# A layer of gated linear attention and a four-layer FFN: the order of TensorE's work at the end of a half, and how sums of squares are formed

## The reference, cut to what matters

```python
xn = _layernorm(x)                                   # x: 16 x 512 x 256
x = x + attn(xn) + ffn(xn)

# attn (Di = 512, K = 64)
u = xn @ up_w.T ; final_gate = xn @ gate_w.T
shift = silu(causal_conv4(u) + conv_b)
q, k = shift @ q_w.T, shift @ k_w.T
o = gla_chunk_scan(q * SCALE, kn, v, rt_log)         # gated linear attention
o = o + shift * residual_weight
xg = o * silu(final_gate)
rms = rsqrt(mean(xg * xg, axis=-1) + 1e-5)
attn = (xg * rms * norm_weight) @ down_w.T           # 512 -> 256

# ffn (ternary weights, 256 -> 1024 -> 1024 -> 1024 -> 256)
h = silu(xn @ w1.T * s1) * (xn @ w2.T * s2)
h = gelu(h @ h1.T * sh1)
h = gelu(h @ h2.T * sh2)
ffn = h @ w3.T * s3
```

## Time and profile before

| | us |
|---|---|
| median of 3 runs | 1945.26 (1943.17 to 1946.41) |
| the profiled execution | 1944.75 |
| its span on the core | 1943.0 |
| TensorE busy | 1926.5 (99%) |
| VectorE busy | 1586.9 (82%) |
| ScalarE busy | 1296.4 (67%) |
| GpSimd busy | 81.2 (4%) |
| one half in the loop | about 58.9 |

### The profile page before, as it was taken

The page is one execution under the profiler, slowest core; times in us unless marked ns, Lnnn a source line. Parts: engine busy times, 40 slices in busy tenths (PEclk is TensorE's granted clock), DMA queues, the critical chain, the costliest instruction groups (busy, mean ns, idle before and its releaser), DMA issues.

```text
span 1943.0 us, 46120 instructions
## 1 busy us (share of the span) xinstructions
PE 1926.5 (99%) x16804; PEld 1907.6 (98%) x16804; DVE 1586.9 (82%) x4304; ACT 1296.4 (67%) x2687; POOL 81.2 (4%) x136
## 2 busy tenths in 40 slices
PE   8999999999999999999999999999999999999998
PEld 7999999999999999999999999999999999999998
DVE  7788888888788887888888788787888878878887
ACT  5676667766676766666766677675667666667565
POOL 0000000000000000000000000000000000000000
PEclk9999999999999999999999999999999999999999
DMA  8000000000000000000000000000000000000000
GB/s 308 7 12 12 12 2 12 12 12 12 12 1 12 12 12 12 11 2 12 12 12 12 7 7 12 12 12 12 1 12 12 12 12 12 1 12 12 13 7 8
DMA packets 23538, 34.19 MB, mean 18 GB/s; under 512 B 3170, under 2 KB 19810, under 8 KB 23364
## 3 DMA queue, kind: packets, MB, share of 16 engines
q1 hardware_dynamic: 23364, 31.43, 4.8%
HBM read 23.04 MB, written 8.39 MB: 16 GB/s over the span
## 4 chain that ended last, share of the span: by engine, by line
PE 95%; issue 2%; ACT 1%; DVE 1%; SPq 1%; DMA 0%; POOLq 0%; POOL 0%; DVEq 0%; ACTq 0%
PE fb L383 65%; PE ab L383 21%; PE ab L593 2%; PE ab L628 1%; PE ab L529 1%; PE ab L518 1%; PE ab L453 1%; PE ab L583 1%; PE fb L679 1%; SPq L289 0%; PE ab L590 0%; PE ab L469 0%; ACT wwhole L727 0%; PE ab L606 0%; DMA shift<-stage_w 0%
## 5 line engine op out<-in xcount | busy, mean ns | idle before, releaser
L383 PE MATMUL fb<-hid1h,wwhole 128*128 128x256 f32 x2048 | 474.7, 279 | 0.0
L383 PE MATMUL fb<-hid1l,wwhole 128*128 128x256 f32 x2048 | 468.5, 276 | 0.0
L383 PE MATMUL fb<-hid0l,wwhole 128*128 128x256 f32 x2048 | 465.9, 276 | 0.0
L383 PE MATMUL fb<-hid0h,wwhole 128*128 128x256 f32 x2048 | 465.8, 276 | 0.0
L383 PEld LDWEIGHTS fb<-hid1h,wwhole 128*128 128x128 f32 x2048 | 384.6, 188 | 3.9 <-ACT raw L839 0.2
L383 PEld LDWEIGHTS fb<-hid1l,wwhole 128*128 128x128 f32 x2048 | 384.7, 188 | 0.0
L383 PEld LDWEIGHTS fb<-hid0h,wwhole 128*128 128x128 f32 x2048 | 384.4, 188 | 0.0
L383 PEld LDWEIGHTS fb<-hid0l,wwhole 128*128 128x128 f32 x2048 | 384.4, 188 | 0.0
L839 ACT ACTIVATE raw<-fb,sh_s 128x256 f32<-128x256 f32 x512 | 212.9, 466 | 143.2 <-PE fb L383 135.1
L383 PE MATMUL fb<-xntl,wwhole 128*128 128x256 f32 x1024 | 237.5, 276 | 0.0
L383 PE MATMUL fb<-xnth,wwhole 128*128 128x256 f32 x1024 | 237.5, 276 | 0.0
(11 more groups left out here) (234 smaller groups left out, 4527.3 us busy)
## 6 DMA issues: line engine op xcount, KB each, us to landing
xin<-x SPq DMA_DIRECT2D x32, 256.0 KB, 2.6
out<-xin SPq DMA_DIRECT2D x32, 256.0 KB, 2.2
stage_more<-stage_w SPq DMA_DIRECT2D x6, 512.0 KB, 7.3
sgate<-stage_w SPq DMA_DIRECT2D x4, 512.0 KB, 4.7
shift<-stage_w SPq DMA_DIRECT2D x4, 512.0 KB, 5.4
v<-stage_w SPq DMA_DIRECT2D x4, 512.0 KB, 5.6
raw<-stage_w SPq DMA_DIRECT2D x3, 512.0 KB, 6.1
mixed<-stage_w SPq DMA_DIRECT2D x3, 512.0 KB, 8.4
```

The lines of the kernel that those rows point to most:

```text
L383: mm = pe.matmul(o, a, b, start=start and i == 0, stop=stop and i == len(pairs) - 1)
```

## The change

On TensorE w3 goes directly behind h2. The four transposes of the next input follow it, and behind them, in the same group, two new transposes that bring `sqsum` (128 features by 128 tokens, twice) to 128 tokens by 128 features in `fb[1]`. The two matmuls with ones behind the down projection are gone. VectorE sums what the two transposes leave over the free dimension (`total`), and forms `msq` from that.

On ScalarE the squares are formed in two pieces of 128x512, ahead of `ln_high`. On VectorE three additions take the place of the reduction over the four squares, and they stand ahead of `ln_low`; `total` and `msq` come ahead of the products with `s3`; the final multiply-add waits for the down projection by itself.

```diff
-                if not (last and p == HALVES - 1):
-                    ln_transpose(me)
-
                 for k in range(FB):
...
                 mm.then_inc(w3_mm.sem, 1)
 
+                if not (last and p == HALVES - 1):
+                    ln_transpose(me)
+                pe.wait_ge(sqsum_d.sem, sqsum_d.at(me))
+                pe.wait_ge(gelu2_d.sem, gelu2_d.at(me, 4))
+                for c in range(NC):
+                    mm = pe.transpose(fb[1][:, c * P:(c + 1) * P], sqsum[:, c * CH:(c + 1) * CH], ident_s[:])
+                mm.then_inc(rs_mm.sem, 1)
+
                 pe.wait_ge(xg_hi.sem, xg_hi.at(me))
...
                 mm.then_inc(dn_mm.sem, 1)
-                pe.wait_ge(sqsum_d.sem, sqsum_d.at(me))
-                pe.wait_ge(gelu2_d.sem, gelu2_d.at(me, 4))
-                for c in range(NC):
-                    mm = pe.matmul(fb[1][:, c:c + 1], sqsum[:, c * CH:(c + 1) * CH], ones[:, 0:1], start=True, stop=True)
-                mm.then_inc(rs_mm.sem, 1)
...
+                for d in (0, 2):
+                    act.activation(sq[:, d:d + 2, :], sgate[:, d:d + 2, :], ACT.Square).then_inc(sq_d.sem, 1)
                 if not (last and p == HALVES - 1):
                     ln_high(me)
-
-                act.activation(sq[:], sgate[:], ACT.Square).then_inc(sq_d.sem, 1)
...
                 hidden_low(hid0l, hid0h, 3, hid2_hi, hid2_lo)
+                for d in (0, 2):
+                    dve.wait_ge(sq_d.sem, sq_d.at(me, d // 2 + 1))
+                    dve.tensor_tensor(sq[:, d, :], sq[:, d, :], sq[:, d + 1, :], ALU.add).then_inc(sqsum_d.sem, 1)
+                dve.wait_ge(sqsum_d.sem, sqsum_d.at(me, 2))
+                dve.tensor_tensor(sqsum, sq[:, 0, :], sq[:, 2, :], ALU.add).then_inc(sqsum_d.sem, 2)
                 if not (last and p == HALVES - 1):
                     ln_low(me)
-                dve.wait_ge(sq_d.sem, sq_d.at(me))
-                dve.tensor_reduce(sqsum, sq.rearrange("p d t -> p t d"), mybir.AxisListType.X, ALU.add).then_inc(sqsum_d.sem, 1)
+                dve.wait_ge(rs_mm.sem, rs_mm.at(me))
+                dve.tensor_reduce(total[:], fb[1][:, 0:NC * P].rearrange("p (c k) -> p c k", c=NC), mybir.AxisListType.X,
+                                  ALU.add).then_inc(total_d.sem, 1)
+                dve.wait_ge(total_d.sem, total_d.at(me))
+                dve.tensor_scalar(msq[:], total[:], 1.0 / DI, EPS, ALU.mult, ALU.add).then_inc(msq_d.sem, 1)
...
-                dve.wait_ge(rs_mm.sem, rs_mm.at(me))
-                dve.tensor_scalar(msq[:], fb[1][:, 0:NC], 1.0 / DI, EPS, ALU.mult, ALU.add).then_inc(msq_d.sem, 1)
                 dve.wait_ge(fin_d.sem, fin_d.at(me, 3))
                 dve.wait_ge(rms_d.sem, rms_d.at(me))
+                dve.wait_ge(dn_mm.sem, dn_mm.at(me))
```

More of the change, by code:

```diff
@@ L184, in layer_program @@
         ssk, rkn = sb("ssk", [P, NC]), sb("rkn", [P, NC])
-        msq, rms = sb("msq", [P, NC]), sb("rms", [P, NC])
+        msq, rms, total = sb("msq", [P, NC]), sb("rms", [P, NC]), sb("total", [P, NC])
         later_k, earlier_q = sb("later_k", [P, 1]), sb("earlier_q", [P, 1])
@@ L219, in layer_program @@
         gelu1_d, hid1_hi, gelu2_d, hid2_hi = sig("gelu1_d", FB), sig("hid1_hi", 4), sig("gelu2_d", FB), sig("hid2_hi", 4)
-        sq_d, xg_hi, ln_hi = sig("sq_d", 1), sig("xg_hi", 1), sig("ln_hi", 1, 1)
+        sq_d, xg_hi, ln_hi = sig("sq_d", 2), sig("xg_hi", 1), sig("ln_hi", 1, 1)
         conv_d, l1_d, hid0_lo, shift_lo = sig("conv_d", DB * (W - 1)), sig("l1_d", FB), sig("hid0_lo", 4), sig("shift_lo", 1)
@@ L233, in layer_program @@
         o_d, xg_d, xg_lo = sig("o_d", 2, 2), sig("xg_d", 1), sig("xg_lo", 1)
-        sqsum_d = sig("sqsum_d", 1)
+        sqsum_d, total_d = sig("sqsum_d", 4), sig("total_d", 1)
         hid1_lo, hid2_lo = sig("hid1_lo", 4), sig("hid2_lo", 4)
```

## The result

The changed kernel is slower: median 1957.07 us of 4 runs (1956.45 to 1957.33), against 1945.34 (1943.17 to 1946.41, 4 runs) for the kernel before on the same chip; ratio 1.006, 95% interval 1.0048 to 1.0072. The forecast was 1935.8 with a range of 1931.8 to 1940.8. The span of the profiled execution grew by 12.2 us, from 1943.0 to 1955.2.

A forecast was written before the change was run, and what follows sets the result against it. The prediction took TensorE, busy 1926.5 of 1943.0 us, as the bound. Savings of 8.7 us (.28 us in each of 31 halves) and 0.8 at the end, 9.5 in all, gave 1935.8 us from the median 1945.26; range 1931.8 to 1940.8.

The forecast's parts named there:

- three things: In the loop: TensorE's queued instructions, the distance between starts, and the few microseconds behind its last instruction.
- Rival D: Behind down: without the sums of squares, slow spacing runs through the next 100 matmuls; 14 us, 1949.8; chance .07.
- slow spacing: w3 and down behind a transpose group: matmul starts 117.7 to 117.9 ns apart instead of 113.3 to 113.4.
- The queue, .28 us a half: TensorE's stretch from w3 to the next half: 7.11 us against 7.40 and 7.39; times 31, 8.7 us.
- 3.63, .57, .20 and 2.71: TensorE's costs per half in us: w3, six transposes, the long first step behind them, the rest of down.
- B: Down behind six transposes: runs at 113.3 ns, 3.3 us more gain, 1932.5; chance 0.14.
- C: w3: spacing doesn't hang on what stood ahead, stays at 117.7 ns; 4.3 us less gain, 1940.1; chance 0.09.
- E: Squares' transposes: the sum comes 0.1 to 0.3 us late each half; 3 to 9 us back, 1939 to 1945; chance 0.10.
- The end of the program: Last half: VectorE's final multiply-add waits only for down and starts near 1938.0, 0.8 us earlier.

The follow-up runs named there:

- e2: Changed kernel with 24 more TensorE instructions (satisfied waits) ahead of the loop; 1945.06 us, ratio 1.0001.
- e5: Changed kernel with 56 fewer TensorE instructions ahead of the loop (warm-up matmuls left out); 1950.09 us, ratio 1.003.
- e6: Kernel before with 40 fewer TensorE instructions ahead of the loop (warm-up matmuls left out); 1984.9 us, ratio 1.0209.
- e8: Changed kernel with the squares' two transposes and their waits moved behind down; 1946.82 us, ratio 1.0011.
- e14: e4 with two transposes of the squares behind down in place of the matmuls with ones, VectorE summing what they leave; 1943.94 us, ratio .9992.
- e16: e4 with two transposes of the squares added directly ahead of the matmuls with ones, results unused; 1951.27 us, ratio 1.0041.
- e4: Kernel before with w3 ahead of the input transposes, and square and reduction ahead of the next input; 1941.63 us, ratio .9982.
- e13: e4 with ScalarE's two squares and VectorE's three adds, the matmuls with ones kept; 1943.61 us, ratio .9992.
- e17: e4 with VectorE's sum over fb[1] added, its result unused; 1943.47 us, ratio .999.
- e12: Changed kernel with four unused plain float32 matmuls of one column behind down in every half; 1970.84 us, ratio 1.013.
- e10: Changed kernel with 24 more TensorE instructions ahead of the loop, one float32 matmul behind down in second halves, 100 satisfied waits ahead of VectorE's loop; 1948.57 us.
- e3: Kernel before with 56 fewer TensorE instructions ahead of the loop (warm-up matmuls left out); 1947.85 us, ratio 1.0013.
- e7: Changed kernel with one unused plain float32 matmul of one column behind down in every half; 1959.93 us, ratio 1.008.

## Why the prediction was wrong, point by point

- **"... inside the loop TensorE never waits, and only three things can move the time."** This is the step that failed. It was true of the kernel before and was taken for a property of the program. A fourth thing, the sequencer's lead over the array, was not in the sum: it was 2.0 us at the back edge with a branch of .7, and the change pushed the branch to 2.25. That cost 9.7 us, shown by e2, e5, e6 and e8. Nor did the prediction name what is queued behind the wait that it moved ahead of down: the rest of the iteration, the branch and the fetch.
- **Rival D, "nothing ends the slow spacing any more".** The direction was right and the place was not. The 100 matmuls named run at 113 ns in the changed kernel. (e2 has three first halves of the form that D describes, .5 us each, but e6 has four with the sums of squares in place.) The slow spacing sits in the projection, h1 and h2, some 250 matmuls, behind the transposes of `xbuf`, and only in some first halves. It cost 9.5 us, D had .07 of the chance, and e14 and e16 against e4, e13 and e17 lay it to the squares' transposes. The prediction had read from rows 6 and 11 that such a stretch recovers; in 10 of 16 first halves it didn't. That the sums of squares "end" the slow spacing was read from one stretch; the changed kernel's z and up are at 113 ns without them, and with them or their like e12 and e16 have slow layers.
- **The queue, .28 us a half.** The pieces came to the hundredth: 3.63, .57, .20 and 2.71 forecast, 3.64, .57, .20 and 2.71 measured. (The .57 is right as a sum and partly by luck: priced at .36 and .21, the first four take .43 and the two of the squares .14.) The stretch of 7.40 us became 7.12. But the saving over 30 halves is 5.9 us, not 8.4, mostly because in every second iteration of the kernel before, 8 of 15, the fast spacing came back within w3 of the first half; such a half took 58.75 instead of 58.98. The earlier trace rows is one of the seven others. One window per kind of half was too few, and that a group of transposes "leaves TensorE in a slower spacing that lasts through w3 and down" was true of 23 of the 31 groups of the kernel before.
- **B and C.** C is false: w3 runs at 113.4 once it follows h2. B is false for most halves: down stays at 118 ns behind the six transposes in 23 of 31. In the other 8, all of them slow first halves, it runs at 113, as B had it.
- **E, the squares late for TensorE.** The array never waits for them in the loop, the third add ends .2 us ahead, as worked out. But their lateness for the sequencer is what cost time.
- **The end of the program.** .8 us forecast, 1.1 measured.
- **The half behind the loop.** 1.3 us that the prediction lacked. They hang on the place of VectorE's code (e10), so probably on its own fetch.

## What to carry to other kernels

Before moving a wait, ask how far the sequencer is ahead of its engine at the next branch, and read the branch's own duration and the instruction queue's packets there: an engine that is 99% busy can still have its lead cut short. Any edit, even of instructions that run once ahead of a loop, moves the places of the blocks; so measure a change at two or three shifts before believing a difference of 1% or less. And compare all repetitions of a stretch, not one window, where the same instructions come at two spacings.

## What the runs showed of the hardware

- A loop's branch on TensorE's sequencer took .36 us, .5 to 1.4, 2.25 or 3.4 us (medians) for nearly the same loop, by where a 16 KB packet of instructions falls and by what holds the sequencer; it ended 2.3 to 2.9 us after that packet's start, in 17 profiles. It took .36 where no packet lies ahead of it (e3, e5).
- 40 instructions less ahead of a loop cost 40 us (2.1%) in 15 iterations; 24 more gave 12 us back in the changed kernel.
- The same 128 matmuls take 14.51 or 15.08 us at the same granted clock (the top one). Behind the eight transposes of `xbuf` the spacing starts at 118 to 120 ns and in most halves comes back to 113 after some five matmuls. With two more transposes at the end of the half before, it didn't in 48 of 176 first halves; without them in 0 of 112, and in 1 of 16 with the large gap of e6.
- Plain float32 matmuls of one column show as two records each: one put the next matmul back by .13 us (e7), two by .36, four by .80 (e12).
